# Image 0's statistics of x read through twelve buffers instead of four, group 0 kept in the ring, parameters issued by ACT, image 1's first counting moved into image 0

## The chip, the cores and the metric

The kernel runs on one core of a Trainium2 chip. The metric is the device time of the program in microseconds (us); lower is better. Times inside the program are us from the start of the profiled span.

## What is computed

```
x  [8 images, 128 channels, 256 x 256] f32
x1 = x + pointwise(shift(groupnorm(x)))          # groups of 4 channels, statistics per image
x2 = x1 + block(groupnorm(x1))                   # wavelet split, 1x1, GELU, depthwise 3x3,
                                                 # norm, two 1x1, 1x1, GELU, wavelet join
```

`shift` moves each channel by its own fraction of a pixel in y and x (four bilinear neighbours). The first group norm needs mean and variance of a whole image of x before the first row of that image can be shifted. The rest of the network does not matter here beyond this: everything behind the first layer follows it in order.

## The kernel before, in words

Channels lie on the 128 partitions. An image is cut into 32 chunks of 8 rows (1 MB, `CH` = 2048 elements per partition), taken in 8 groups (`NG`) of 4 (`SLOTS`). Every x is read twice: once for its statistics, into the four buffers `ahead[s]`, and once for the shift, into the four slots of `ring`, which hold 34 rows (one halo row above and below).

- **Counting.** DVE counts three quarters of a chunk with three `bn_stats` (`count_x`, L1056) and raises `x_counted`. ACT sums the last quarter and its squares (`sum_x`, L556 and L557) and raises `x_summed`. `load_x_ahead` (SP, L333) waits for both before it reuses a buffer, so at most four chunks are under way.
- **Scales.** `x_moments` (L1076 to 1086) joins the sums and raises `mom_ready` at L1085; PE takes the mean over the groups (`channel_means`, L767); DVE makes the variance (`group_variance`, from L1091), ACT its square root (L499), DVE the scales (`x_scales`) and from them the two scaled weight matrices (`x_weights`, L1111 and L1112), which release PE through `shift_ready`.
- **Shift.** A step of `shift_rows` on DVE handles one chunk with three passes of 128x2048: L1163 (row above), L1177 (row below, raises `u_done`), L1192 (column left, raises `v_done`). PE (`conv`) multiplies u by the weights for the column to the right (L782, needs `u_done` and x put into PSUM) and then v (L787, needs `v_done`), half a chunk at a time. ACT's step (`shift_group`) is: the next image's `sum_x`; `take_x1` of half 0 (L530, PSUM to SBUF with sums); `put_x` of the next chunk's half 0 (L508); the same for half 1, with the store of x1 (L538) between; a sum of squares (L546).
- **The next image.** While image b is shifted, DVE and ACT count image b+1, one chunk a step: group g counts group g+1 of the next image, and the last group counts group 0 of image b+2. So two things stand ahead of image 0: the statistics of image 0 (32 chunks), and the counting of group 0 of image 1 (4 chunks).
- **Orders written out by hand.** Each engine has one instruction stream, in program order. SP: 19 parameter loads (L327, all counted by `params_in`), 32 `load_x_ahead` of image 0, the four ring loads of group 0 (`load_ring`, L342), four `load_x_ahead(1, 0, s)`, then `load_image(0)`, which begins with four `load_x_ahead(1, 1, s)` and goes on with a ring load and a `load_x_ahead` per step. A ring load of slot s waits until DVE has finished u of the chunks that read the slot (`u_done`: of the next chunk too, for s < 3; of slot 3 itself for s = 3), and until ACT has put the chunk into PSUM. DVE: it waits for all parameters and for POOL's constants, does 23 small setup steps (L1022 to 1045), counts image 0, makes the moments, counts group 0 of image 1, makes the scales and starts image 0. `x_weights` comes in step 1 of image 0. ACT: sums of image 0, square root, first `put_x`, sums of group 0 of image 1, image 0. PE primes its PSUM banks after the setup and then waits for `shift_ready`.

DVE's stream between the last count of image 0 and image 0 itself reads:

```
x_moments(0, 1)
for s in range(SLOTS):
    count_x(1, 0, s)
group_variance(1, gmom_x, ps_small_x)
x_scales(1)
```

Of the kernel before, what the change touches and what calls it, by code (L numbers as in the profile page):

```python
# [45 lines left out]
def preact_kernel(nc, x, theta_s, w_dw, w_pwT, w_c1T, b_c1, bn1_g, bn1_b, dw_w, dw_b, gn_g, gn_b,  # L46
# [5 lines left out]
    with ExitStack() as ctx:  # L52
# [212 lines left out]
        cov_ready, cov_done = sem("cov_ready"), sem("cov_done")  # L265
        slot_in = [sem(f"slot_in{s}") for s in range(SLOTS)]
        ahead_in = [sem(f"ahead_in{s}") for s in range(SLOTS)]
        x1_loaded = [sem(f"x1_loaded{s}") for s in range(SLOTS)]
        bias0_ready = sem("bias0_ready")
        u_up, v_done, v_left = sem("u_up"), sem("v_done"), sem("v_left")  # L270
# [24 lines left out]
        def nth(t, back=0):  # L295

            return t + (1 + LEAD - back)

        def three_in_v(b, s):

            return final(b) and s % 2 == 1
# [21 lines left out]

        @block.sync
        def _(sp):
            for dst, src in PARAMS:
                sp.dma_start(dst, src).then_inc(params_in, 16)  # L327

            def load_x_ahead(b, g, s):

# [41 lines left out]
                    if beyond:  # L373
                        load_x_ahead(b + 2, 0, s)

            with sp.Fori(0, NG) as g:
                for s in range(SLOTS):
                    load_x_ahead(0, g, s)
            for s in range(SLOTS):
                load_ring(0, 0, s, first=True)  # L380
            for s in range(SLOTS):
                load_x_ahead(1, 0, s)
            load_image(0, before=False, tail=False, following=True, beyond=True)
            load_image(1, before=True, tail=False, following=True, beyond=True)
            with sp.Fori(2, B - 2) as b:
                load_image(b, before=True, tail=True, following=True, beyond=True)
# [103 lines left out]
        def _(act):  # L490
# [57 lines left out]
            def sum_x(b, g, s):  # L548

                q = b * NCH + g * SLOTS + s  # L550
                act.wait_ge(ahead_in[s], b * (16 * NG) + g * 16 + 16)

                wait_alone(act, nth(q, 1), x_summed)
                piece = ahead[s][:, DVE_PIECES * BANK:]
                i = g * SLOTS + s
                nc.scalar.activation(x_copy, piece, ACT.Identity, accum_out=sums_x[:, 0, bass.ds(i, 1)])  # L556
                nc.scalar.activation(x_squares, piece, ACT.Square,  # L557
                                     accum_out=sums_x[:, 1, bass.ds(i, 1)]).then_inc(x_summed, 1)
# [43 lines left out]

            def image(b, before, tail, following, beyond):

                shift_group(b, 0, before, tail, (b + 1, 1) if following else None, "first")
                with act.Fori(1, NG - 1) as g:
                    shift_group(b, g, before, tail, (b + 1, g + 1) if following else None, "")
                shift_group(b, NG - 1, before, tail, (b + 2, 0) if beyond else None, "last")

            with act.Fori(0, NG) as g:  # L610
                for s in range(SLOTS):
                    sum_x(0, g, s)
            square_root(1)
            act.wait_ge(primed, 1)
            for half in range(2):
                put_x(0, 0, 0, half)
            for s in range(SLOTS):
                sum_x(1, 0, s)
            image(0, before=False, tail=False, following=True, beyond=True)
            image(1, before=True, tail=False, following=True, beyond=True)  # L620
            with act.Fori(2, B - 2) as b:
# [363 lines left out]
        def _(dve):  # L985
# [63 lines left out]

            def count_x(b, g, s, pieces=range(DVE_PIECES)):  # L1050

                if 0 in pieces:
                    dve.wait_ge(ahead_in[s], b * (16 * NG) + g * 16 + 16)
                i = g * SLOTS + s
                for r in pieces:
                    last = nc.vector.bn_stats(stats_x[:, bass.ds(i * (6 * DVE_PIECES) + 6 * r, 6)],  # L1056
                                              ahead[s][:, r * BANK:(r + 1) * BANK])
                if DVE_PIECES - 1 in pieces:
                    last.then_inc(x_counted, 1)

# [83 lines left out]
            def shift_rows(b, g, s, before, tail, ahead_of, place):  # L1144

                t = b * NCH + g * SLOTS + s
                k = s % 2
                first, last = place == "first", place == "last"
                nx, n1 = b * 2 + 2, b * 2 + 1
                for near in range(s, min(s + 2, SLOTS)):  # L1150
                    dve.wait_ge(slot_in[near], b * (16 * NG) + g * 16 + 16)

                dve.wait_ge(conv_done, nth(t * 2 + 1, 4))
                if first and s == 0:
                    pad_columns(0)
                    done(pad_row(0))
                if first and s == 1:
                    done(pad_columns(1))
                    x_weights()
                if last and s == 0:  # L1160
                    done(pad_row(SLOTS * ROWS + 1))
                u = u_buf[k][:, :, 1:W + 1]
                stt(out=u, in0=ring[:, s * ROWS:(s + 1) * ROWS, :], scalar=up, in1=slot(s),  # L1163
                    op0=ALU.mult, op1=ALU.add).then_inc(u_up, 1)
                late = last and s == 0
                if first and s == 1:

                    dve.wait_ge(x1_ready, nth(b * (2 * NCH), 1))
                    x_bias(1 if isinstance(b, int) and b == 0 else b * 2)
                if first and s == 2 and before:  # L1170
                    group_variance(n1, gmom, ps_small)
                if last and s == 2 and not final(b):
                    group_variance(nx, gmom_x, ps_small_x)
                if ahead_of and not late:
                    count_x(*ahead_of, s, range(0, 2))
                dve.wait_ge(u_up, t + 1)
                stt(out=u, in0=ring[:, s * ROWS + 2:(s + 1) * ROWS + 2, :], scalar=down, in1=u,  # L1177
                    op0=ALU.mult, op1=ALU.add).then_inc(u_done, 1)
                if first and s == 1 and before:
                    x1_moments(b - 1)  # L1180
                if late:
                    keep_first(b)
                if ahead_of and not late:
                    count_x(*ahead_of, s, range(2, DVE_PIECES))
                if before and not three_in_v(b, s):
                    if not first:
                        count_y1(b - 1, g - 1, s)
                    elif tail:
                        count_y1(b - 2, NG - 1, s)
                dve.wait_ge(u_done, nth(t))  # L1190
                v = v_buf[k].rearrange("p (r c) -> p r c", c=W)
                left_added = stt(out=v, in0=u_buf[k][:, :, 0:W], scalar=left, in1=u, op0=ALU.mult, op1=ALU.add)  # L1192
                if three_in_v(b, s):
                    left_added.then_inc(v_left, 1)
                    if before:
                        count_y1(b - 1, g - 1, s) if not first else count_y1(b - 2, NG - 1, s)
                    dve.wait_ge(v_left, g * 2 + (s // 2 + 1))
                    stt(out=v, in0=u_buf[k][:, :, 2:W + 2], scalar=right, in1=v,
                        op0=ALU.mult, op1=ALU.add).then_inc(v_done, 1)
                else:  # L1200
                    left_added.then_inc(v_done, 1)
                if late and not final(b):
                    x_moments(b + 1, nx)
                if ahead_of and late:
                    count_x(*ahead_of, s)
                if last and s == 2 and not final(b):
                    x_scales(nx)
                if first and s == 2 and before:
                    x1_scales(n1)
                if first and s == 3 and before:  # L1210
                    c1_weights(b - 1, n1)

            def image(b, before, tail, following, beyond):

                for s in range(SLOTS):
                    shift_rows(b, 0, s, before, tail, (b + 1, 1) if following else None, "first")
                with dve.Fori(1, NG - 1) as g:
                    for s in range(SLOTS):
                        shift_rows(b, g, s, before, tail, (b + 1, g + 1) if following else None, "")
                for s in range(SLOTS):  # L1220
                    shift_rows(b, NG - 1, s, before, tail, (b + 2, 0) if beyond else None, "last")

            with dve.Fori(0, NG) as g:
                for s in range(SLOTS):
                    count_x(0, g, s)
            start_steps(SETUP_STEPS)
            x_moments(0, 1)
            for s in range(SLOTS):
                count_x(1, 0, s)
            group_variance(1, gmom_x, ps_small_x)  # L1230
            x_scales(1)
            IMAGE_STEPS = 27
            image(0, before=False, tail=False, following=True, beyond=True)
            start = SETUP_STEPS + steps[1]
# [246 lines left out]
```

## Time and profile before

| | |
|---|---|
| median of 3 runs | 5441.45 us (5440.20 to 5441.63) |
| profiled execution, its own time | 5440.21 us |
| its span, first to last instruction | 5438.6 us |
| mean granted TensorE clock | 0.964 |
| busy: PE, DVE, ACT, POOL | 88%, 86%, 77%, 19% of the span |
| HBM read, written | 946.55 MB, 662.70 MB |
| first parameter issued; first x load issued | 0.95 us; 10.33 us |
| transfers issued by ACT: stores of x1, stores of y1 | 256 of 1 MB, 128 of 512 KB |
| last chunk of image 0 counted | 96.00 us |
| first shift pass of image 0; of its group 1 | 119.56 us; 158.51 us |

The time of a run is a little more than the span, which counts from the first to the last instruction. Busy shares are over the whole program; the change touches the first 160 us or so, so the shares are read by windows and by the timeline.

### The profile page before, as it was taken

To read this page: it belongs to the slowest core of one execution; us is meant where nothing else is said; L and a number is where in the kernel's file an instruction comes from. 1 tells how busy PE (TensorE), PEld (TensorE's weight loads), DVE (VectorE), ACT (ScalarE), POOL (GpSimd) and SP (SyncE) were. 2 spreads that over 40 slices of the span, in tenths; PEclk is the share of its full clock that TensorE was granted. 3 is DMA by queue.
4 is the path that set the end of the run, shared out by engine and by line. 5 is a ranking of instruction groups with operands and counts; after the bars stand their busy time and mean duration, and the time that the engine had idled before them with its cause. 6 is when DMAs were issued, how large, how long until landed. Compare 5 with 4: busy or idle time off the path is not lost.

```text
span 5438.6 us, 54871 instructions
## 1 busy us (share of the span) xinstructions
PE 4778.1 (88%) x12740; PEld 2174.6 (40%) x12740; DVE 4686.9 (86%) x4430; ACT 4166.8 (77%) x5706; POOL 1047.0 (19%) x743
## 2 busy tenths in 40 slices
PE   0889999999999999999998999999997777777775
PEld 0334444444444444444443555555552222222222
DVE  6999898898988989889937999999659888888887
ACT  4887777777777777777736788888659888888887
POOL 0000000000000000000004888888501111111111
PEclk6999999999999999999999999999999999999998
DMA  8999999999999999999993333333239999999999
GB/s 346 363 358 411 426 425 425 416 426 426 415 426 416 426 426 417 426 397 373 398 330 125 124 128 128 132 130 129 75 76 221 235 236 236 236 235 236 236 236 223
DMA packets 256302, 1610.79 MB, mean 296 GB/s; under 512 B 30256, under 2 KB 30640, under 8 KB 92336
## 3 DMA queue, kind: packets, MB, share of 16 engines
q1 hardware_dynamic: 164016, 1005.35, 46.8%
q0 software_dynamic: 36864, 268.45, 23.8%
q10 hardware_dynamic: 55296, 335.57, 14.8%
q8 instruction: 48, 0.79, 0.1%
q14 instruction: 78, 0.64, 0.0%
HBM read 946.55 MB, written 662.70 MB: 296 GB/s over the span
## 4 chain that ended last, share of the span: by engine, by line
PE 43%; DMA 23%; DVE 17%; issue 9%; ACT 4%; DVEq 0%; ACTq 0%; POOLq 0%; SPq 0%; POOL 0%
DMA out_x<-arena 19%; PE ps L799 14%; PE ps L787 11%; PE ps L782 10%; PE ps L870 4%; DMA arena<-in_x 3%; DVE arena L1290 2%; DVE arena L1177 2%; ACT arena L744 2%; DVE arena L1314 2%; DVE arena L1163 2%; PE ps L917 2%; DVE arena L1192 2%; DVE arena L1427 2%; DVE ps L1303 1%
## 5 line engine op out<-in xcount | busy, mean ns | idle before, releaser
L972 PE MATMUL ps<-arena,c2T 128*128 128x512 f32 x2048 | 1025.9, 652 | 365.9 <-ACT arena L737 363.6
L787 PE MATMUL ps<-arena 128*128 128x512 f32 x2048 | 964.4, 595 | 24.4 <-DVE arena L1192 24.4
L799 PE MATMUL ps<-arena 128*128 128x512 f32 x2048 | 963.7, 614 | 15.2 <-DVE small L1141 13.1
L782 PE MATMUL ps<-arena 128*128 128x512 f32 x1920 | 913.0, 598 | 42.9 <-DVE arena L1112 22.9
L453 POOL TENSOR_SCALAR arena<-arena,taps 128x1024 f32<-128x1024 f32 x238 | 265.9, 1117 | 2914.5 <-ACT arena L650 2882.0
L530 ACT ACTIVATE arena<-ps,small 128x1024 f32<-128x1024 f32 x512 | 567.6, 1109 | 321.5 <-PE ps L787 320.9
L972 PEld LDWEIGHTS ps<-arena,c2T 128*128 128x128 f32 x2048 | 401.5, 205 | 989.6 <-ACT arena L737 560.9
L737 ACT ACTIVATE arena<-ps,small 128x512 f32<-128x512 f32 x1024 | 713.1, 778 | 99.8 <-DVE arena L1419 91.1
L1163 DVE SCALAR_TENSOR_TENSOR arena<-arena,shift 128x2048 f32<-128x2048 f32 x256 | 601.2, 2348 | 199.8 <-DMA arena<-in_x 149.9
L1303 DVE SCALAR_TENSOR_TENSOR ps<-arena,taps,ps 128x512 f32<-128x512 f32 (+1 forms) x604 | 683.2, 1177 | 21.3 <-PE ps L917 20.7
L508 ACT ACTIVATE ps<-arena 128x1024 f32<-128x1024 f32 x512 | 526.3, 1028 | 169.5 <-ACT arena L530 159.6
L1177 DVE SCALAR_TENSOR_TENSOR arena<-arena,shift 128x2048 f32<-128x2048 f32 x256 | 598.2, 2337 | 1.4
L799 PEld LDWEIGHTS ps<-arena 128*128 128x128 f32 x2048 | 383.1, 189 | 540.8 <-issue 534.8
L787 PEld LDWEIGHTS ps<-arena 128*128 128x128 f32 x2048 | 386.9, 190 | 529.6 <-issue 475.4
L1192 DVE SCALAR_TENSOR_TENSOR arena<-arena,shift 128x2048 f32<-128x2048 f32 x256 | 597.8, 2335 | 0.6
L744 ACT ACTIVATE arena<-arena 128x2048 f32<-128x2048 f32 x256 | 490.1, 1915 | 112.6 <-DVE arena L1427 110.7
L782 PEld LDWEIGHTS ps<-arena 128*128 128x128 f32 x1920 | 360.8, 190 | 521.6 <-issue 448.3
L1056 DVE BATCH_NORM_STATS2 arena<-arena 128x512 f32 (+1 forms) x768 | 498.9, 682 | 29.7 <-DMA arena<-in_x 29.4
L1426 DVE TENSOR_TENSOR arena<-arena 128x1024 f32<-128x1024 f32 x256 | 314.4, 1228 | 209.9 <-DMA out_x<-arena 208.7
L546 ACT ACTIVATE arena<-arena 128x2048 bf16<-128x2048 f32 x256 | 484.8, 1894 | 0.4 <-ACT arena L530 0.4
L481 POOL DMA_DIRECT2D out_x<-arena x256 | 218.1, 852 | 1321.8 <-ACT arena L744 1288.5
L467 POOL TENSOR_TENSOR arena<-arena 128x1024 f32<-128x1024 f32 x128 | 302.5, 2364 | 129.6 <-ACT arena L686 70.8
(167 smaller groups left out, 5409.3 us busy)
## 6 DMA issues: line engine op xcount, KB each, us to landing
arena<-in_x SPq DMA_DIRECT2D x400, 1024.0 KB, 16.0
out_x<-arena ACTq DMA_DIRECT2D x256, 1024.0 KB, 9.0
arena<-out_x SPq DMA_DIRECT2D x256, 1024.0 KB, 17.0
out_x<-arena POOLq DMA_DIRECT2D x256, 1024.0 KB, 17.0
arena<-in_x SPq DMA_DIRECT2D x112, 1152.0 KB, 15.5
y_dram<-arena ACTq DMA_DIRECT2D x128, 512.0 KB, 8.6
arena<-y_dram SPq DMA_DIRECT2D x128, 512.0 KB, 3.6
h_dram<-arena SPq DMA_DIRECT2D x112, 512.0 KB, 2.7
```

The lines of the kernel that those rows point to most:

```text
L508: nc.scalar.activation(banks(half), ring[:, bass.ds(1 + s * ROWS + half * 4, 4), :] .rearrange("p r c -> p (r c)"), ACT.Copy).then_inc(x_i ...
L530: nc.scalar.activation(x1_buf[k][:, half * (CH // 2):(half + 1) * (CH // 2)], banks(half), ACT.Identity, bias=bias0, accum_out=total).then ...
L737: last = nc.scalar.activation(g_buf[k][:, q, :], ps[:, 4 * k + q, :], ACT.Gelu, bias=z_bias[:, q:q + 1], scale=z_scale[:, q:q + 1])
L744: nc.scalar.activation(y_buf[s], y_buf[s], ACT.Copy, scale=0.5).then_inc(y_ready, 1)
L782: mm(ps[:, r, :], w_right[:, :], u_buf[k][:, 2 * r:2 * r + 2, 2:W + 2], start=False, stop=False, skip_group_check=True)
L787: last = mm(ps[:, r, :], w_center[:, :], v_buf[k][:, r * BANK:(r + 1) * BANK], start=False, stop=True, skip_group_check=True)
L799: last = mm(ps[:, 4 + s % 2, :], w_c1b[:, q, :], cells[:, q // 2, q % 2, :, :], start=(q == 0), stop=(q == 3))
L972: last = mm(ps[:, 4 * k + q, :], c2T[:, q, :], h2[:, k * HC:(k + 1) * HC], start=True, stop=True)
L1163: stt(out=u, in0=ring[:, s * ROWS:(s + 1) * ROWS, :], scalar=up, in1=slot(s), op0=ALU.mult, op1=ALU.add).then_inc(u_up, 1)
L1177: stt(out=u, in0=ring[:, s * ROWS + 2:(s + 1) * ROWS + 2, :], scalar=down, in1=u, op0=ALU.mult, op1=ALU.add).then_inc(u_done, 1)
L1192: left_added = stt(out=v, in0=u_buf[k][:, :, 0:W], scalar=left, in1=u, op0=ALU.mult, op1=ALU.add)
L1303: stt(out=acc, in0=h_tile(t, dy, dx, first), scalar=tap_weight(dy, dx), in1=acc, op0=ALU.mult, op1=ALU.add).then_inc(dw_acc, 1)
```

## The change

- SP no longer issues the parameters; ACT issues the same 19 transfers ahead of its first `sum_x`. SP begins with x.
- The 32 chunks of image 0 go to twelve buffers. Group 0 is loaded into the ring's slots, counted there and stays for the shift. Odd groups go to `ahead[s]`, even groups from 2 on to `x1_in[s]`, which image 0 does not use otherwise, with new semaphores `first_in[s]`. From group 3 on a load waits until the chunk 8 places before it has been counted by DVE and ACT. The later reload of the ring's group 0 is gone.
- The loops over image 0's chunks are unrolled on SP, ACT and DVE.
- Group 0 of image 1 is counted in the steps of group 0 of image 0. Group 1 of image 1 is counted in a block of its own between group 0 and group 1 of image 0, four chunks on DVE and four on ACT. From group 1 on all is as before.
- SP's order at that place is: ring(0, 1, s) and ahead(1, 1, s) in turn for four s, then ahead(1, 2, s) for four s, then as before.
- For image 0, `x_weights` stands right behind `x_scales`, ahead of step 0.

```diff
@@ helpers
+        def first_chunk(g, s):
+            if g == 0:
+                return slot(s).rearrange("p r c -> p (r c)"), slot_in[s], 16
+            return (ahead[s], ahead_in[s], g * 8 + 8) if g % 2 else (x1_in[s], first_in[s], g * 8)
+
+        def ahead_count(b, g):
+            return b * (16 * NG) + g * 16 + (16 - 16 * (NG // 2))
@@ SP
-            for dst, src in PARAMS:
-                sp.dma_start(dst, src).then_inc(params_in, 16)
...
-            with sp.Fori(0, NG) as g:
-                for s in range(SLOTS):
-                    load_x_ahead(0, g, s)
-            for s in range(SLOTS):
-                load_ring(0, 0, s, first=True)
+            def load_first_image():
+                for s in range(SLOTS):
+                    load_ring(0, 1, s)
+                    load_x_ahead(1, 1, s)
+                for s in range(SLOTS):
+                    load_x_ahead(1, 2, s)
+                with sp.Fori(2, NG - 1) as g:
+                    for s in range(SLOTS):
+                        load_ring(0, g, s)
+                        load_x_ahead(1, g + 1, s)
+                for s in range(SLOTS):
+                    load_ring(0, NG - 1, s, last=True)
+                    load_x_ahead(2, 0, s)
+
+            for t in range(NCH):
+                g, s = t // SLOTS, t % SLOTS
+                if g == 0:
+                    load_ring(0, 0, s, first=True)
+                    continue
+                chunk, arrived, _ = first_chunk(g, s)
+                if g > 2:
+                    wait_alone(sp, nth(t, 2 * SLOTS), x_counted, x_summed)
+                sp.dma_start(chunk, x[0, :, t * CH:(t + 1) * CH]).then_inc(arrived, 16)
             for s in range(SLOTS):
                 load_x_ahead(1, 0, s)
-            load_image(0, before=False, tail=False, following=True, beyond=True)
+            load_first_image()
@@ ACT
-                shift_group(b, 0, before, tail, (b + 1, 1) if following else None, "first")
+                first_image = isinstance(b, int) and b == 0
+                shift_group(b, 0, before, tail, (b + 1, 0 if first_image else 1) if following else None, "first")
+                if first_image:
+                    for s in range(SLOTS):
+                        sum_x(1, 1, s)
...
-            with act.Fori(0, NG) as g:
-                for s in range(SLOTS):
-                    sum_x(0, g, s)
+            for dst, src in PARAMS:
+                act.dma_start(dst, src).then_inc(params_in, 16)
+            for t in range(NCH):
+                sum_x(0, t // SLOTS, t % SLOTS)
             square_root(1)
             act.wait_ge(primed, 1)
             for half in range(2):
                 put_x(0, 0, 0, half)
-            for s in range(SLOTS):
-                sum_x(1, 0, s)
@@ DVE
                 if first and s == 1:
                     done(pad_columns(1))
-                    x_weights()
+                    if not (isinstance(b, int) and b == 0):
+                        x_weights()
...
-                    shift_rows(b, 0, s, before, tail, (b + 1, 1) if following else None, "first")
+                    shift_rows(b, 0, s, before, tail, (b + 1, 0 if first_image else 1) if following else None, "first")
+                if first_image:
+                    for s in range(SLOTS):
+                        count_x(1, 1, s)
...
-            with dve.Fori(0, NG) as g:
-                for s in range(SLOTS):
-                    count_x(0, g, s)
+            for t in range(NCH):
+                count_x(0, t // SLOTS, t % SLOTS)
             start_steps(SETUP_STEPS)
             x_moments(0, 1)
-            for s in range(SLOTS):
-                count_x(1, 0, s)
             group_variance(1, gmom_x, ps_small_x)
             x_scales(1)
+            x_weights()
```

`sum_x` and `count_x` take buffer, semaphore and count from `first_chunk` for image 0 and the count from `ahead_count` for the others.

## Rows read from the trace of the kernel before

**Rows 1.** Windows of core 0: us, busy of each engine (count), granted clock, DMA share, GB/s.

```profile
50.00:75.00 25.00, 0.00 (x0) 0.00 (x0) 18.94 (x32) 16.40 (x45) 0.00 (x0) 0.50 1.01 421
...
175.00:200.00 25.00, 21.59 (x48) 8.61 (x48) 25.00 (x19) 22.30 (x36) 0.00 (x0) 1.00 0.99 368
...
600.00:800.00 200.00, 198.52 (x461) 86.20 (x461) 182.88 (x178) 154.33 (x247) 0.00 (x0) 1.00 1.01 425
```

**Rows 2.** Timeline, first 40 us: start, length, engine, line, operation, [idle before <-releaser].

```profile
0.95 0.39 SPq L327 DMA_DIRECT2D theta<-in_theta_s  x1
...
9.45 0.43 SPq L327 DMA_DIRECT2D bn<-in_bn_b  x1
10.33 29.91 SPq L333 DMA_DIRECT2D arena<-in_x  x13
11.49 0.15 DVE L1022 TENSOR_SCALAR small<-theta 128x1 f32<-128x1 f32 x1 [11.49 <-DMA bn<-in_bn_b]
...
15.65 1.28 ACT L556 ACT_TABLE_LOAD   x1 [15.65 <-DMA arena<-in_x]
...
18.82 7.22 DVE L1056 BATCH_NORM_STATS2 arena<-arena 128x512 f32 x12 [0.35 <-DVE gram L1045]
```

**Rows 3.** Timeline, 85 to 140 us, from the last counted chunk to the first output.

```profile
94.12 1.88 DVE L1056 BATCH_NORM_STATS2 arena<-arena 128x512 f32 x3 [0.61 <-DMA arena<-in_x]
...
99.41 0.16 DVE L1085 SCALAR_TENSOR_TENSOR small<-small,part 128x2 f32<-128x2 f32 x1
...
115.94 0.14 DVE L1091 COPY small<-ps 128x2 f32<-128x2 f32 x1
...
119.56 2.35 DVE L1163 SCALAR_TENSOR_TENSOR arena<-arena,shift 128x2048 f32<-128x2048 f32 x1
...
132.27 3.78 PE L782 MATMUL ps<-arena 128*128 128x512 f32 x4 [12.68 <-DVE arena L1112]
...
137.84 1.11 ACT L530 ACTIVATE arena<-ps,small 128x1024 f32<-128x1024 f32 x1 [11.37 <-PE ps L787]
```

**Rows 4.** Chain of waits in order of time, 86 to 160 us: start, length, what.

```profile
120.14 4.86 DMA arena<-in_x
...
136.05 1.75 PE ps L787 x4
...
149.95 2.34 DVE arena L1163
...
158.51 2.34 DVE arena L1163
```

**Rows 5.** Parameter transfers (L327), issued 1 to 10 us: time to landing.

```profile
DMA to landing us min/median/max: 1.9/2.1/2.8
```

**Rows 6.** DMA queues in 802.5 to 804.5 us, image 1: packets, MB, share of 16 engines.

```profile
q1 hardware_dynamic: 76, 0.55, 65.1%
q10 hardware_dynamic: 77, 0.32, 38.3%
```

**Rows 7.** The page, DMA queues over the whole span: packets, MB, share of 16 engines.

```profile
q10 hardware_dynamic: 55296, 335.57, 14.8%
```

**Rows 8.** Loads of 512 KB on SP, 2900:4000 alone, 4300:5300 beside q0: landing.

```profile
arena<-y_dram SPq DMA_DIRECT2D x122, 512.0 KB, 3.6
...
q0 software_dynamic: 25916, 188.72, 90.8%
q1 hardware_dynamic: 12954, 47.17, 12.5%
...
arena<-h_dram SPq DMA_DIRECT2D x90, 512.0 KB, 10.2
```

**Rows 9.** ACT in the timeline at 161.65 us: the fourth sum of group 0.

```profile
161.65 0.61 ACT L556 ACTIVATE arena<-arena 128x512 bf16<-128x512 f32 x1
```

**Rows 10.** L333 loads issued at 148.0 and at 163.2 us: time to landing.

```profile
DMA to landing us min/median/max: 8.1/8.1/8.1
...
DMA to landing us min/median/max: 12.7/12.7/12.7
```

More of the change, by code:

```diff
@@ L267, in preact_kernel @@
         ahead_in = [sem(f"ahead_in{s}") for s in range(SLOTS)]
+        first_in = [sem(f"first_in{s}") for s in range(SLOTS)]
         x1_loaded = [sem(f"x1_loaded{s}") for s in range(SLOTS)]
@@ L550, in sum_x @@
                 q = b * NCH + g * SLOTS + s
-                act.wait_ge(ahead_in[s], b * (16 * NG) + g * 16 + 16)
+                chunk, arrived, count = first_chunk(g, s) if isinstance(b, int) and b == 0 else \
+                    (ahead[s], ahead_in[s], ahead_count(b, g))
+                act.wait_ge(arrived, count)
                 wait_alone(act, nth(q, 1), x_summed)
-                piece = ahead[s][:, DVE_PIECES * BANK:]
+                piece = chunk[:, DVE_PIECES * BANK:]
                 i = g * SLOTS + s
@@ L1050, in count_x @@
             def count_x(b, g, s, pieces=range(DVE_PIECES)):
+                chunk, arrived, count = first_chunk(g, s) if isinstance(b, int) and b == 0 else \
+                    (ahead[s], ahead_in[s], ahead_count(b, g))
                 if 0 in pieces:
-                    dve.wait_ge(ahead_in[s], b * (16 * NG) + g * 16 + 16)
+                    dve.wait_ge(arrived, count)
                 i = g * SLOTS + s
@@ L1056, in count_x @@
                     last = nc.vector.bn_stats(stats_x[:, bass.ds(i * (6 * DVE_PIECES) + 6 * r, 6)],
-                                              ahead[s][:, r * BANK:(r + 1) * BANK])
+                                              chunk[:, r * BANK:(r + 1) * BANK])
                 if DVE_PIECES - 1 in pieces:
@@ L1213, in image @@
             def image(b, before, tail, following, beyond):
+                first_image = isinstance(b, int) and b == 0
                 for s in range(SLOTS):
-                    shift_rows(b, 0, s, before, tail, (b + 1, 1) if following else None, "first")
+                    shift_rows(b, 0, s, before, tail, (b + 1, 0 if first_image else 1) if following else None, "first")
+                if first_image:
+                    for s in range(SLOTS):
+                        count_x(1, 1, s)
                 with dve.Fori(1, NG - 1) as g:
```

## The prediction, written before the changed kernel had run

> **What bounds the kernel now.** I read the windows first. While image 0 is counted, the DMA engines are full (share 1.01, 421 GB/s) and DVE works 18.94 of 25 us; while it is shifted, DVE is busy 25.00 of 25 us; from image 1 on the DMA is full again and sets the pace [rows 1]. Every later stage follows the end of the head in order, with the same transfers and buffers, so what the head gains or loses I carry to the end one for one. The head is read in the timeline. SP issues its first x at 10.33 us, behind 19 parameters issued from 0.95 us at 0.47 us each; DVE leaves the wait for the parameters at 11.49 us, sets up for 7.33 us and begins to count at 18.82 us [rows 2]. The last chunk is counted at 94.12 + 1.88 = 96.00 us, the moments are out at 99.57 us. Then DVE waits for four chunks of image 1 and counts them, and the variance comes only at 115.94 us, the first shift pass at 119.56 us [rows 3]. Step 0 then waits until 125.00 us for a load issued at 120.14 us; group 1 of image 0 begins at 158.51 us [rows 4]. I forecast that last mark; call it G1.
>
> **The order behind the count.** T0 is the first shift pass. After the change it follows the last count by: moments 99.57 - 96.00 = 3.57; PE's group mean and its hand-over, which no row of mine shows alone, 0.7 (not under 0.1, and not over the 0.95 of one cold matmul record of 512 columns, 3.78 / 4 [rows 3], as it has two columns); variance, root, scales and pads 119.56 - 115.94 = 3.62 [rows 3]; the two weight matrices, each 128x128, 0.4 (under one 128x512 count of 0.60, 7.22 / 12 [rows 2], apiece). That is 8.3 us, where it took 23.56. So the order by itself gives back 15.3 us: the reload of ring and image 1's counting have left the path.
>
> **From T0 to G1.** Before: 158.51 - 119.56 = 38.95 us. Steps are 8.56 us (158.51 - 149.95 [rows 4]). After: four steps and 0.7 of pads and bias, 34.9 us, without the wait for the load (image 1's group 0 is issued as image 0's last group is counted, and has all of the 8.3 us and 2.4 more). Then the new block of four counts on DVE, 4 x 3 x 0.60 = 7.2 us. That would be G1 = T0 + 42.1. But look at who lets the fourth chunk of it be loaded. Load ahead(1, 1, 3) waits for ACT's sum of (1, 0, 3), the first thing in ACT's step 3. ACT's first drain comes 5.9 us (two passes and two counts) after T0 for u, then 3.78 us of cold matmuls and 1.75 us of warm ones [rows 3, 4]: T0 + 11.4. From first drain to the fourth sum it took 161.65 - 137.84 = 23.8 us, the sum itself 1.2 [rows 3, 9]; with some waits for v instead of a backlog I take 26. So the load is issued at T0 + 37.5, when DVE stands at 34.9. Ahead of it on SP's queue are ring(0, 1, 2), ahead(1, 1, 2) and ring(0, 1, 3), all let go at the end of step 3, beside a store of x1. Such loads took 8.1 us from issue to landing with little before them and 12.7 in just this crowd [rows 10]; I take 10.5. It lands at T0 + 48, is counted in 1.9: G1 = T0 + 50, with ends 46.5 and 52.5, and 42.1 only if the load came without wait. Compared with 38.95 this half loses 11 us of the 15.3.
>
> **The start of the stream.** Moving the parameters lets x start about 9 us sooner: first issue near 1.3 instead of 10.33. If nothing else happened, the stream would end near 87 us instead of 94.1: earlier by 9.0, less some 2 us for parameter bytes and packets that now share the engines. DVE needs 32 x 1.805 = 57.8 us for its counts, so it stays hidden if it begins by about 30, which asks for the parameters by 23 us. They land within 2.8 us of issue now, with empty queues [rows 5]. Issued by ACT from about 1.5 to 10 us, they meet twelve 1 MB loads that SP issues in the same 6 us without any wait. What do the engines do then? They are spared this by the twelve buffers running out: after 12 x 2.49 us (1 MB at 421 GB/s [rows 1]) there is no x left to load until DVE counts, and DVE counts nothing until the parameters are in. First landing 1.3 + 5.3 (15.65 - 10.33 [rows 2]), the twelfth 27.4 later, 2 for the parameters between, 1 to 2 for the seven left over: the parameters are in at about 37 us, not 11.49.
>
> The Trainium skill ("DMA: Bandwidth & Descriptors", Queues, rings and completion order) says that an engine drains a whole packet of 9 to 17 descriptors from one queue before it turns to the next. Equal bursts would fit rows 6 too; with 17 of the small against 9 of the large, the parameters would be in some 7 us sooner, and the sum below would be that much lower. The sum goes by one for one.
>
> Then: setup 7.33, DVE starts at 44.3. Chunk 12 waits for five chunks counted (44.3 + 9.0), is issued at 53.6 and lands 5 to 6 us later, 59. Nineteen more at 2.49: 106.3. Counted: 108.2 us, against 96.0. The DVE bound, 44.3 + 57.8 = 102.1, lies below. So the new start costs 12.2 us where it was to give 8. ACT's own sums (1.5 us a chunk against 2.49) and PE's priming stay covered.
>
> **Sum.** T0 = 108.2 + 8.3 = 116.5. G1 = 166.5, against 158.51: 8.0 us later. Behind G1: ahead(1, 2, 0) is issued near T0 + 46 and wanted at T0 + 52.4; with 5 us it lands at 51, at no cost. The profiled execution goes from 5440.21 to 5448.2; it lies 1.24 us below the median of the three runs, from which the same sum gives 5449.4. I say 5449. What the measurement can tell from no change is about 0.2%, 10.9 us, so this is no change by that bound. Its own range: parameters 33 to 39, landing 8.1 to 12.7, gives 5443 to 5455.
>
> **Rivals.**
> 1. *Parameters pass quickly.* If small packets slip through, or the first of them get ahead of the x loads and the rest take a few us, they are in before 23 us; DVE is hidden, the last chunk is counted at 88, T0 = 96.3, G1 = 146.3: 12 us faster, 5429. For it: they land in 2 us now [rows 5]. Against it: rows 6 and 8. Chance 0.20. If the fourth load also cost nothing, 5421.
> 2. *Late parameters, no stall at the fourth load.* G1 = 116.5 + 42.1 = 158.6, 5441 to 5443. For it: the DMA has slack in the steps before, while 34.9 against 37.5 is a narrow gap on ACT. Against it: the 12.7 of rows 10. Chance 0.17.
> 3. *The stall goes on into group 1.* The block's sums on ACT let go ahead(1, 2, 0) only at T0 + 46; if it too takes 12.7 us behind the fourth load and the store of chunk 3, it lands at 58.7 where DVE wants it at 52.4. Price 6.3 us, so 14 in all: 5456. It decides once that landing takes more than 6.4 us. For it: both landings of rows 10 are longer than that. Against it: by then nothing else of SP's is queued, since ring(0, 2, 0) waits for step 1 of group 1. Chance 0.14.
> 4. *The change does not do what it says.* Twelve buffers bring nothing to the rate, as the DMA is full with four [rows 1]; that is in the sum already.
>
> **How the numbers follow.** The forecast gets 0.47, rivals 1 to 3 get 0.20, 0.17 and 0.14; 0.02 is elsewhere. The range goes from 5428, to take in most of rival 1, to 5456, to take in rival 3. Faster by over 0.2% (below 5430.6): rival 1 and a little, 0.21. Slower by over 0.2% (above 5452.3): rival 3 and the top end of the forecast, 0.20. The rest is 0.59: forecast and rival 2.
>
> **What would show it.** Right: first DVE setup step (L1022 before) near 37 us instead of 11.49, idle on the parameters; a hole in DMA from about 37 to 54 us; last chunk of image 0 counted near 108; first shift pass near 116; a DVE wait of 5 to 8 us for x in the block between groups 0 and 1; G1 near 166. Wrong: a first setup step before 23 us, and the last count near 88 us; or a block that takes 7.2 us flat. If G1's shift is not the shift of the end, the idea that the DMA-bound images carry it one for one is wrong.

## The result and the profile after

The changed kernel takes 5456.11 us (median of 9 runs, 5449.55 to 5457.76) against 5441.63 (9 runs, 5436.00 to 5446.03) for the kernel before: ratio 1.0025, 95% interval 1.0015 to 1.0036. It is slower by 14.5 us between the medians. The forecast was 5449 with a range up to 5456, so the median lies at the very top of the range, and beyond the 0.2% inside which I had put most of the chance. The profiled execution took 5452.45 us, span 5450.8, that is 12.2 us more than before. Three executions in the slow state, two of e2 (6375 and 8127 us) and one of e4 (9230 us), are left out of the ratios below.

The marks of the forecast, read in both traces and in those of the experiments. "Setup" is DVE's first setup step, "counted" the end of the last count of image 0, T0 the first shift pass, G1 the first shift pass of group 1.

| kernel | setup | counted | T0 | G1 | G1 - T0 | span |
|---|---|---|---|---|---|---|
| before | 11.49 | 96.00 | 119.56 | 158.51 | 38.95 | 5438.6 |
| forecast for the change | 37 | 108.2 | 116.5 | 166.5 | 50 | |
| after | 38.60 | 109.96 | 118.20 | 171.60 | 53.40 | 5450.8 |
| e1, parameters on SP | 11.49 | 94.8 | 103.05 | 157.62 | 54.57 | 5437.2 |
| e2, setup late | late | 98.6 | 106.85 | 159.90 | 53.05 | 5439.1 |
| e3, block in x1_in | 38.73 | 109.7 | 117.98 | 159.84 | 41.86 | 5437.9 |
| e4, before with parameters on ACT | 19.22 | 103.6 | 127.18 | 166.43 | 39.25 | 5448.2 |
| e5, e1 and e3 | 11.50 | 94.8 | 103.02 | 144.89 | 41.87 | 5425.0 |
| e6, spread, late, x1_in | late | 91.5 | 99.75 | 141.62 | 41.87 | 5422.6 |
| e7, half packets | 39.16 | 112.4 | 120.66 | 174.52 | 53.86 | 5455.9 |
| e8, weights late | 38.81 | 110.0 | 117.84 | 172.79 | 54.95 | 5454.5 |
| e9, ahead first | 38.73 | 110.3 | 118.48 | 164.92 | 46.44 | 5451.0 |
| e10, as e6, setup earlier | late | 90.3 | 98.54 | 140.41 | 41.87 | 5419.6 |

("Counted" is the start of the aggregation of the moments less 0.31 us, its distance from the last count in the kernels before and after. "Late": the setup stands behind chunk 20 or 23. The marks are of one profiled execution each.)

The span moves with G1 to within some 2 us in every kernel but one: in e9 G1 is 6.4 us later than in the kernel before and the end 12.4, because a further wait of 4.4 us stands behind G1.

**The start.** The timeline of the kernel after, first 60 us, answers to [rows 2]:

```profile
2.04 0.41 ACTq L644 DMA_DIRECT2D theta<-in_theta_s  x1
...
7.04 1.80 ACTq L644 DMA_DIRECT2D gn<-in_gn_g  x1
...
11.43 3.48 ACTq L644 DMA_DIRECT2D pw1T<-in_pw_wT  x1
...
31.06 2.21 ACTq L644 DMA_DIRECT2D bn<-in_bn_b  x1
33.41 1.28 ACT L585 ACT_TABLE_LOAD   x1 [33.41 <-issue]
...
38.60 0.15 DVE L1054 TENSOR_SCALAR small<-theta 128x1 f32<-128x1 f32 x1 [38.60 <-DMA bn<-in_bn_b]
...
45.62 14.93 DVE L1090 BATCH_NORM_STATS2 arena<-arena 128x6 f32<-128x512 f32 x25
```

SP issues x at 1.43 us, but DVE's first setup step waits until 38.60 us for the last parameter. The first nine of ACT's issues take 0.4 to 0.9 us each; from the tenth on all but one take 1.8 to 6.5 us, and ACT's first sum, with its table load, comes at 33.41. The DMA view of 2 to 40 us gives the time from issue to landing:

```profile
arena<-in_w_c1T ACTq DMA_DIRECT2D x1, 256.0 KB, 15.3
...
theta<-in_theta_s ACTq DMA_DIRECT2D x1, 1.0 KB, 7.6
wdw<-in_w_dw ACTq DMA_DIRECT2D x1, 0.5 KB, 10.1
...
taps<-in_dw_w ACTq DMA_DIRECT2D x1, 4.5 KB, 23.4
...
gn<-in_gn_b ACTq DMA_DIRECT2D x1, 0.5 KB, 27.7
...
bn<-in_bn_b ACTq DMA_DIRECT2D x1, 2.0 KB, 7.5
```

These answer to [rows 5], where none took over 2.8 us. Issue and landing time together put theta at 9.6 us, the second parameter at 12.6, the fourth at 19.2, the eighth (taps) at 29.4: 2.5 to 3.5 us apart, where I had put 2.8. The eleventh is in at 36.6, the last at 38.6. And the two queues between 20 and 30 us, for [rows 6]:

```profile
q1 hardware_dynamic: 566, 4.13, 99.4%
q10 hardware_dynamic: 565, 0.01, 3.4%
```

566 packets against 565, while the one moves 4.13 MB and the other 0.01. The hole in the DMA that I had forecast from 37 to 54 us comes as well, until SP issues the next x load (chunk 12) at 54.72 us:

```profile
40.00:50.00 10.00, 4.36 (x5) 1.85 (x6) 9.41 (x34) 9.19 (x29) 0.00 (x0) 1.00 0.01 2
```

**Behind the count**, for [rows 3]:

```profile
108.08 1.88 DVE L1090 BATCH_NORM_STATS2 arena<-arena 128x6 f32<-128x512 f32 x3 [0.60 <-DMA arena<-in_x]
...
114.21 0.16 DVE L1125 COPY small<-ps 128x2 f32<-128x2 f32 x1 [0.68 <-PE ps L799]
...
118.20 2.35 DVE L1198 SCALAR_TENSOR_TENSOR arena<-arena,shift 128x2048 f32<-128x2048 f32 x1
```

From the last count (109.96) to T0 8.24 us.

**The block between groups 0 and 1**, in the timeline and, below it, the landing of the load issued at 155.92 us, for [rows 10]:

```profile
150.19 0.33 SPq L349 DMA_DIRECT2D arena<-in_x  x1
...
151.03 0.33 SPq L340 DMA_DIRECT2D arena<-in_x  x1
...
152.94 3.65 DVE L1090 BATCH_NORM_STATS2 arena<-arena 128x6 f32<-128x512 f32 x6
...
155.92 16.19 SPq L340 DMA_DIRECT2D arena<-in_x  x5
...
162.17 1.88 DVE L1090 BATCH_NORM_STATS2 arena<-arena 128x6 f32<-128x512 f32 x3 [5.58 <-DMA arena<-in_x]
...
169.80 1.88 DVE L1090 BATCH_NORM_STATS2 arena<-arena 128x6 f32<-128x512 f32 x3 [5.75 <-DMA arena<-in_x]
...
171.60 2.34 DVE L1198 SCALAR_TENSOR_TENSOR arena<-arena,shift 128x2048 f32<-128x2048 f32 x1
...
173.85 1.28 DVE L1090 BATCH_NORM_STATS2 arena<-arena 128x512 f32 x2
```

```profile
DMA to landing us min/median/max: 13.9/13.9/13.9
```

DVE counts two chunks at once, waits 5.58 us for the third and 5.75 for the fourth, which was issued at T0 + 37.7 and took 13.9 us to land. Group 1 itself has no such wait. The windows of that stretch, for [rows 1]:

```profile
155.00:160.00 5.00, 3.49 (x9) 1.22 (x7) 1.58 (x3) 4.17 (x9) 0.00 (x0) 1.00 1.00 405
160.00:165.00 5.00, 0.00 (x0) 0.00 (x0) 1.88 (x3) 4.75 (x9) 0.00 (x0) 0.57 1.01 429
165.00:170.00 5.00, 0.00 (x0) 0.00 (x0) 0.20 (x1) 2.18 (x9) 0.00 (x0) 0.50 1.00 423
```

The DMA is full for all 15 us and DVE works 3.66 of them.

### The profile page after: what moved, and what is told of

It is laid out like the page before. It is cut to its first block, busy times and chain, and to the rows that moved or that the text cites. A ratio compares the mean times of both kernels' runs of the same rounds, so it can differ in the third digit from the quotient of the medians.

```text
span 5450.8 us, 54465 instructions
## 1 busy us (share of the span) xinstructions
PE 4783.9 (88%) x12740; PEld 2177.6 (40%) x12740; DVE 4684.9 (86%) x4430; ACT 4156.7 (76%) x5699; POOL 1046.9 (19%) x743
## 3 DMA queue, kind: packets, MB, share of 16 engines
q1 hardware_dynamic: 160704, 1000.41, 46.4%
## 4 chain that ended last, share of the span: by engine, by line
PE 42%; DMA 24%; DVE 19%; issue 10%; ACT 3%; ACTq 1%; DVEq 0%; POOLq 0%; SPq 0%; POOL 0%
DMA out_x<-arena 19%; PE ps L831 13%; PE ps L819 10%; PE ps L814 10%; DMA arena<-in_x 4%; PE ps L902 4%; DVE arena L1212 3%; DVE arena L1327 2%; DVE arena L1198 2%; DVE arena L1351 2%; ACT arena L776 2%; DVE arena L1090 2%; PE ps L949 2%; DVE arena L1464 2%; DVE arena L1227 2%
## 5 line engine op out<-in xcount | busy, mean ns | idle before, releaser
L1340 DVE SCALAR_TENSOR_TENSOR ps<-arena,taps,ps 128x512 f32<-128x512 f32 (+1 forms) x604 | 686.2, 1189 | 21.5 <-PE ps L949 20.8
```

Source lines behind the costliest of these rows:

```text
L1340: stt(out=acc, in0=h_tile(t, dy, dx, first), scalar=tap_weight(dy, dx), in1=acc, op0=ALU.mult, op1=ALU.add).then_inc(dw_acc, 1)
```

## The experiments

### e1: the parameters back on SP

```diff
+            for dst, src in PARAMS:                       # SP, ahead of x
+                sp.dma_start(dst, src).then_inc(params_in, 16)
-            for dst, src in PARAMS:                       # ACT
-                act.dma_start(dst, src).then_inc(params_in, 16)
```

> The changed kernel with one part undone: the 19 parameters are issued by SP ahead of x again. Theory (parameters queued behind twelve x loads, one packet for one): first setup step of DVE back at 11.5 us instead of 38.6, x begins at 10.4, last chunk of image 0 counted near 95 instead of 109.96, first shift pass near 103, group 1 of image 0 near 156.5 instead of 171.6. End about 15 us below the changed kernel, about 2 us below the kernel before: 5440. Rival (the parameters do not matter, the late load of the block does): as the changed kernel, 5456.

Measured: 5439.13 us against 5442.83 for the kernel before, run beside it, ratio 0.9994 (0.9985 to 1.0003). The start is back where it was; the stall of the block remains. DVE's timeline:

```profile
11.49 0.15 DVE L1055 TENSOR_SCALAR small<-theta 128x1 f32<-128x1 f32 x1 [11.49 <-DMA bn<-in_bn_b]
...
95.12 2.75 DVE L1115 BATCH_NORM_AGGREGATE small<-arena 128x2 f32<-128x576 f32 x1
...
103.05 2.35 DVE L1199 SCALAR_TENSOR_TENSOR arena<-arena,shift 128x2048 f32<-128x2048 f32 x1
```

```profile
155.82 1.88 DVE L1091 BATCH_NORM_STATS2 arena<-arena 128x6 f32<-128x512 f32 x3 [5.77 <-DMA arena<-in_x]
157.62 2.33 DVE L1199 SCALAR_TENSOR_TENSOR arena<-arena,shift 128x2048 f32<-128x2048 f32 x1
```

T0 is 15.15 us earlier than in the changed kernel, from this one edit, and G1 14.0. This edit alone takes the changed kernel from slower to level with the kernel before (so does e3, by another term).

### e2: DVE counts first and sets up after chunk 23

```diff
-            dve.wait_ge(params_in, 16 * len(PARAMS))
...
             for t in range(NCH):
+                if t == 24:
+                    set_up()
                 count_x(0, t // SLOTS, t % SLOTS)
```

`set_up()` holds the wait for the parameters and the 23 setup steps.

> The changed kernel, but DVE counts first and does its parameter setup only after chunk 23, so that DVE no longer waits for the parameters. Theory A (DVE's wait is the only damage): x never pauses, last count near 89, group 1 at 150.6, end 21 us below the changed kernel: 5435. Theory B (ACT is held as well, because it cannot issue its 19 transfers while the engines are full, and its first sum comes at 33 us or later): x pauses after twelve chunks until ACT has summed five, chunk 12 is issued near 42, last count near 96.5, group 1 near 158, end 13 us below the changed kernel: 5442 to 5444. I hold B for likelier.

Measured: 5443.71 us, ratio 1.0001 (0.9992 to 1.001). Theory B: DVE no longer waits for a parameter, and still a hole comes, from ACT. DVE's timeline around it, and SP's loads issued from 30 to 60 us:

```profile
37.15 1.88 DVE L1092 BATCH_NORM_STATS2 arena<-arena 128x6 f32<-128x512 f32 x3 [0.88 <-DMA arena<-in_x]
46.96 1.88 DVE L1092 BATCH_NORM_STATS2 arena<-arena 128x6 f32<-128x512 f32 x3 [7.93 <-DMA arena<-in_x]
```

```profile
L407 SPq DMA_DIRECT2D arena<-in_x x12: 327/328/328, 42.1 to 58.0; - x12
```

Chunk 12 is issued at 42.1 (forecast 42), after ACT has at last summed five. So the changed kernel is held twice by the parameters: DVE by their landing, ACT by their issue; mending DVE alone gives back 11.7 us of G1's 13.1 and not the 21 that theory A asked for.

### e3: group 1 of image 1 in the idle x1_in buffers

```diff
             for s in range(SLOTS):
                 load_x_ahead(1, 0, s)
+            for s in range(SLOTS):
+                sp.dma_start(x1_in[s], x[1, :, (SLOTS + s) * CH:(SLOTS + s + 1) * CH]).then_inc(first_in[s], 16)
@@ load_first_image
                     load_ring(0, 1, s)
-                    load_x_ahead(1, 1, s)
-                for s in range(SLOTS):
                     load_x_ahead(1, 2, s)
```

The block and `sum_x(1, 1, s)` read `x1_in[s]`; the counts of `ahead_in` behind it are 16 lower.

> The changed kernel, but group 1 of image 1 is loaded into the four x1_in buffers, right behind group 0 of image 1 and before image 0 starts, so the block between groups 0 and 1 finds its data. Theory (the block waits for its third and fourth load): first shift pass unchanged near 118.2, the block takes 7.3 us without a wait, group 1 at T0 + 42.1 = 160.3 instead of 171.6; end 11 us below the changed kernel: 5445. Rival (DMA is short in group 0 anyway and the wait moves to the loads of group 2): group 1 starts at 160 but DVE waits in it, end within 4 us of the changed kernel.

Measured: 5441.55 us, ratio 0.9999 (0.999 to 1.0008); 14.6 us below the changed kernel by the medians, 11.8 by G1, 12.9 by the span. The block, and the first step of group 1 behind it:

```profile
152.72 7.21 DVE L1094 BATCH_NORM_STATS2 arena<-arena 128x6 f32<-128x512 f32 x12
159.84 2.33 DVE L1202 SCALAR_TENSOR_TENSOR arena<-arena,shift 128x2048 f32<-128x2048 f32 x1
162.10 1.28 DVE L1094 BATCH_NORM_STATS2 arena<-arena 128x512 f32 x2
```

No wait in the block and none moved into group 1: the rival falls.

### e4: the kernel before with its parameters on ACT

```diff
-            for dst, src in PARAMS:                       # SP
-                sp.dma_start(dst, src).then_inc(params_in, 16)
+            for dst, src in PARAMS:                       # ACT, ahead of its sums
+                act.dma_start(dst, src).then_inc(params_in, 16)
```

x still goes through four buffers.

> The kernel before with one part of the change alone: the parameters issued by ACT. Only four x loads can be under way. Theory (one packet for one while x is queued, then free): four x loads are done at about 14 us, the parameters are in at about 17 us, DVE counts from about 24.5 instead of 18.82, chunk 4 is issued at 26.5, last count near 100.5 instead of 96.0; end 4 to 5 us above the kernel before: 5446. Rival (small transfers pass quickly): parameters in by 12 to 13 us, last count 95 to 96.5, end within 1 us of the kernel before.

Measured: 5449.20 us against 5442.83, ratio 1.0013 (1.0004 to 1.0022), span 9.6 us over that of the kernel before. The parameters come at 19.22 us (forecast 17), G1 at 166.43 (7.9 us late, where 4.5 was forecast).

```profile
19.22 0.15 DVE L1021 TENSOR_SCALAR small<-theta 128x1 f32<-128x1 f32 x1 [19.22 <-DMA bn<-in_bn_b]
```

One part of the change alone, put into the old kernel, costs 6 to 10 us. The direction is the theory's; its size was set too low: I let the parameters behind the four x loads pass in 3 us, and the last of them is issued only at 15.64 us and takes 3.6 us to land.
### e5: e1 and e3 together

```diff
+                sp.dma_start(dst, src).then_inc(params_in, 16)          # as in e1
+                sp.dma_start(x1_in[s], x[1, :, (SLOTS + s) * CH:(SLOTS + s + 1) * CH]).then_inc(first_in[s], 16)   # as in e3
```

> Both repairs together: parameters on SP ahead of x, and group 1 of image 1 in the x1_in buffers. Theory (the two damages are separate terms that add): first shift pass at 103.1 as with the parameters on SP alone, group 1 at T0 + 42.0 = 145.1, which is 13.4 us ahead of the kernel before; end 5428 to 5430, ratio 0.9975. Rival (they hide one another): end no better than 5436.

Measured: 5427.76 us against 5442.81, ratio 0.9973 (0.9964 to 0.9982). T0 at 103.02, G1 at 144.89 (forecast 145.1). The terms add to within 1 us: e1 takes 14.0 us off G1, e3 11.8, both 26.7.

### e6: parameters one by one between ACT's sums, setup late, x1_in

The edits of e2 and e3, and:

```diff
             for t in range(NCH):
+                if t < len(PARAMS):
+                    act.dma_start(*PARAMS[t]).then_inc(params_in, 16)
                 sum_x(0, t // SLOTS, t % SLOTS)
```

> As the previous run, but the parameters stay on ACT, one issued ahead of each of its first 19 sums, and DVE does its setup after chunk 23. Theory (neither ACT nor DVE waits for a parameter while x flows): x from 1.4 us without a pause, last count near 89, first shift pass near 97.1, group 1 near 139.1, 19 us ahead of the kernel before; end 5422 to 5424. Rival (small transfers beside x cost more than they save): last count after 94, end 5428 or more.

Measured: 5423.74 us against 5442.81, ratio 0.9965 (0.9951 to 0.9979). The time is in the range, the marks are 2.6 us late (T0 99.75, not 97.1). DVE's timeline says why: behind the setup its last eight counts run as one row without a wait,

```profile
68.40 1.88 DVE L1096 BATCH_NORM_STATS2 arena<-arena 128x6 f32<-128x512 f32 x3 [0.61 <-DMA arena<-in_x]
...
77.18 14.34 DVE L1096 BATCH_NORM_STATS2 arena<-arena 128x6 f32<-128x512 f32 x24
```

so the end of the count is DVE's there and not the data's. ACT's issues take 0.33 to 0.40 us each, none is held.

### e7: x in half packets

```diff
-                sp.dma_start(chunk, x[0, :, t * CH:(t + 1) * CH]).then_inc(arrived, 16)
+                sp.dma_start(chunk[:, 0:CH // 2], x[0, :, t * CH:t * CH + CH // 2]).then_inc(half_in[g % 2][s], 16)
+                sp.dma_start(chunk[:, CH // 2:CH], x[0, :, t * CH + CH // 2:(t + 1) * CH]).then_inc(arrived, 16)
```

> The changed kernel, but chunks 4 to 31 of image 0 are loaded as two halves of 4 KB per partition each, so from the fifth chunk on the x packets are half as large and twice as many. In the changed kernel the parameters behind the first few land 2.5 us apart. Theory (one packet for one): behind the first four chunks they land 1.4 to 1.6 us apart and ACT's slow issues shrink in the same ratio; the parameters are in at 32 to 36 us instead of 38.6. Rival (shared by bytes or by time): the spacing does not shrink, parameters in at 38 us or later.

There is one execution: 5457.51 us. The two queues between 20 and 30 us, and two of ACT's issues:

```profile
q1 hardware_dynamic: 1040, 3.79, 96.0%
q10 hardware_dynamic: 1043, 0.10, 8.4%
```

```profile
15.49 1.11 ACTq L648 DMA_DIRECT2D pw2T<-in_pw_wT  x1
16.64 1.10 ACTq L648 DMA_DIRECT2D bpw<-in_pw_b  x1
```

### e8: the weights back in step 1

```diff
-                    if not (isinstance(b, int) and b == 0):
-                        x_weights()
+                    x_weights()
...
             x_scales(1)
-            x_weights()
```

> The changed kernel with x_weights back in step 1 of image 0. Theory (the load of (1, 1, 3) waits for ACT's sum of (1, 0, 3), which follows PE's start): PE starts at T0 + 12.6 instead of T0 + 5.9, ACT's first drain 6 us later, that load is issued near T0 + 43.5 instead of 37.7, group 1 starts near T0 + 59 instead of T0 + 53.4; end 4 to 6 us above the changed kernel. Rival (DMA alone sets the landing, not the issue): group 1 within 1.5 us of T0 + 53.4.

Measured: 5455.32 us, ratio 1.0022 (1.0013 to 1.0032), which cannot be told from the changed kernel. SP's issue of ring(0, 1, 2) and of the fourth chunk's load, DVE's step 2 and the first pass of group 1:

```profile
151.33 0.33 SPq L349 DMA_DIRECT2D arena<-in_x  x1
...
158.59 14.71 SPq L340 DMA_DIRECT2D arena<-in_x  x5
```

```profile
136.93 2.35 DVE L1197 SCALAR_TENSOR_TENSOR arena<-arena,shift 128x2048 f32<-128x2048 f32 x1 [1.01 <-PE ps L819]
...
172.79 2.33 DVE L1197 SCALAR_TENSOR_TENSOR arena<-arena,shift 128x2048 f32<-128x2048 f32 x1
```

In the changed kernel PE starts at T0 + 5.9 and ACT's first drain at T0 + 12.5; here at T0 + 9.5 and T0 + 15.6. (My 12.6 and 6 us were read off the kernel before, whose step 0 held a wait of 3.1 us for a load; that was the error.) The load is issued at T0 + 40.8 instead of 37.7, so ACT's 3.1 us pass on to the issue in full, which is the theory's part. But the load lands in 12.4 us instead of 13.9, and G1 comes at T0 + 54.95, 0.05 us outside what the rival allowed and far from the theory's 59. The 1.55 us that are left need no late issue: DVE itself begins the last pass of step 3 1.5 us later (T0 + 33.98 instead of 32.49), as `x_weights` stands in step 1 and step 2 waits 1.01 us for PE, and ring(0, 1, 2), the first of the loads in front of the fourth, is issued 1.5 us later too (T0 + 33.5 instead of 32.0). Counted from that first issue, the landing does not follow the issue of the fourth load. In us, for the seven traces in which these loads stand in this order:

| kernel | ring(0, 1, 2) issued | fourth load issued, after that | landed, after that |
|---|---|---|---|
| before | 155.91 | 7.3 | 20.0 |
| e4 | 164.24 | 6.9 | 19.4 |
| after | 150.19 | 5.7 | 19.6 |
| e1 | 135.04 | 5.7 | 20.8 |
| e2 | 138.84 | 5.7 | 19.3 |
| e7 | 152.65 | 5.6 | 20.1 |
| e8 | 151.33 | 7.3 | 19.7 |

("Landed" is issue plus landing time in the kernel before and e4, where nothing waits for this load, and the start of DVE's fourth count in the others.) The DMA is full all the while (share 0.98 or more in each half of the stretch), and what is queued from the end of step 3 on sets the landing: with the fourth load issued 5.6 to 7.3 us behind the first, no trace shows an effect of its own of the moment at which ACT lets it go. The early weights, one of the change's parts, gave some 1.2 us at G1 in these two traces, and nothing that the medians show.

### e9: the ahead load before the ring load

```diff
-                    load_ring(0, 1, s)
                     load_x_ahead(1, 1, s)
+                    load_ring(0, 1, s)
```

> The changed kernel, with load ahead(1, 1, s) ahead of ring(0, 1, s) in SP's stream in the first group. Theory (the third and fourth load are late because of what stands before them in SP's queue, and only the fourth because of ACT): the third load is issued near T0 + 29 instead of T0 + 32.8 and lands in time, so its wait of 5.6 us in the block is gone; the fourth is still issued near T0 + 37.5 but without ring(0, 1, 3) before it and lands near T0 + 47; group 1 at T0 + 49 instead of T0 + 53.4; end 4 to 5 us below the changed kernel. Rival (the DMA as a whole is full there, whatever the order): group 1 within 1.5 us of T0 + 53.4, and waits for ring in group 1 if not.

Measured: 5452.47 us against 5442.24, ratio 1.0017 (1.0008 to 1.0026). G1 comes 6.7 us earlier than in the changed kernel (T0 + 46.4, where the theory had 49), but the end only 3.6 by the medians and not at all by the spans, where 4 to 5 were forecast. DVE's timeline:

```profile
163.12 1.88 DVE L1090 BATCH_NORM_STATS2 arena<-arena 128x6 f32<-128x512 f32 x3 [4.47 <-DMA arena<-in_x]
164.92 2.34 DVE L1198 SCALAR_TENSOR_TENSOR arena<-arena,shift 128x2048 f32<-128x2048 f32 x1
171.66 1.28 DVE L1090 BATCH_NORM_STATS2 arena<-arena 128x512 f32 x2 [4.41 <-DMA arena<-in_x]
...
177.97 2.35 DVE L1198 SCALAR_TENSOR_TENSOR arena<-arena,shift 128x2048 f32<-128x2048 f32 x1
```

The third load's wait is gone, and the fourth's is 4.47 us; but step 0 of group 1 now waits 4.41 us for (1, 2, 0), and step 1 starts at 177.97 against 180.15 in the changed kernel. Queue order moves the wait; with the DMA full from 155 to 175 us (share 1.00) it removes only 2.2 us of it. Theory and rival are both right in part. e3, which loads those 4 MB before image 0, removes it all.

### e10: as e6, with the setup after chunk 20

```diff
-                if t == 24:
+                if t == 21:
                     set_up()
```

> As the run with spread parameters and late setup, but the setup stands after chunk 20 instead of chunk 23. There the last eight counts ran back to back on DVE behind the setup and ended at 91.52, later than the data. Theory (those are DVE's, not DMA's): the last count ends near 89.8, first shift pass near 98.0, group 1 near 140.0; end 1.5 to 2 us below the 5423.7 of that run. Rival (the last parameters are not in by then and DVE waits): a DVE wait for a parameter before the setup, end above 5424.

Measured: 5421.98 us against 5442.24, ratio 0.9963 (0.995 to 0.9977), span 19.0 us below that of the kernel before. T0 at 98.54 (1.2 us earlier than e6; 98.0 forecast), G1 at 140.41 (140.0). The ten chunks behind the setup are counted without a wait, and the last one waits 0.60 us for its data, so DVE has just caught up with the stream:

```profile
69.89 17.94 DVE L1096 BATCH_NORM_STATS2 arena<-arena 128x6 f32<-128x512 f32 x30
88.43 1.88 DVE L1096 BATCH_NORM_STATS2 arena<-arena 128x6 f32<-128x512 f32 x3 [0.60 <-DMA arena<-in_x]
```

This is the fastest version tried, 20.3 us below the kernel before beside it; from e6 it is 1.8 us by the medians, with times that overlap (5419.96 to 5423.02 against 5421.21 to 5424.26).

## Why the prediction was right or wrong

**Parameters behind x: right, a little small.** "The parameters are in at about 37 us": 38.60. "Chunk 12 ... issued at 53.6": issued at 54.72, with DVE's first count at 45.62 (44.3). Last count 109.96 against 108.2. Setup 7.02 us to the first count. e1 gives all of it back, e7 shows equal packet counts at another packet size. One step had it too short without effect: SP was to issue the twelve loads in 6 us without a wait, and took from 1.43 to 10.35 us.

The rule of the Trainium skill that I weighed ("DMA: Bandwidth & Descriptors", Queues, rings and completion order: bursts of 9 to 17 descriptors) did not come out apart. Equal counts fit single packets and equal bursts alike, and the 7 us less that I had estimated for unequal bursts did not appear (38.60 us against 37).

**The order behind the count: right.** 8.24 us against 8.3.

**Steps and block without waits: right.** 42.1 forecast, 41.86 in e3, e5, e6 and e10.

**The wait in the block: foreseen, its landing mis-sized.** The step "I take 10.5" for the landing of ahead(1, 1, 3) failed: it was issued at T0 + 37.7 (forecast 37.5) and took 13.9 us, beyond both rows that I had bounded it with. That is 3.4 us and the whole miss of G1 - T0. Of the two rows the 12.7 was the like case: that load stood behind three loads issued in the 7.3 us before it, as here behind three in 5.7 us (the four are 4.2 MB, beside stores of x1). The 8.1 had one load issued just before it. I took the middle between the two. And a landing added to an issue is the wrong form for this term: by e8 and its table the landing follows the start of the crowd, at 19.3 to 20.8 us, and not ACT's sum. I had also overlooked that the third load waits (5.58 us); it cost nothing beyond the fourth's.

That the issue came out at 37.5 against 37.7 is in part luck: ACT's first drain comes at T0 + 12.5 and not 11.4, and from there to the issue it takes 25.2 us and not 26. The ends that I gave, 46.5 and 52.5, do not follow from landings of 8.1 and 12.7, which give 47.5 and 52.1; nor does 5455 for the upper end of the sum, which comes to 5454.

**The sum.** Forecast +8.0 at G1, measured +13.1: 1.7 from the start (118.20 against 116.5), 3.4 from the landing. The span carries 12.2 of it to the end and the medians 14.5; the profiled execution is one of the shorter ones of the nine. That the shift of G1 passes on one for one holds to some 2 us in all kernels but e9.

**The rivals.** Rival 1 (parameters pass quickly) and rival 2 (no stall) did not come. Rival 3 gave the time that was measured, 5456, by another way: group 1 of the changed kernel has no wait for (1, 2, 0). That wait exists, 4.41 us, but only in e9, where the fourth load comes early enough to uncover it. Rival 4 is borne out as far as e1 shows it: with the parameters on SP, twelve buffers end the count at 94.8 us against 96.0. The chance that I gave to "slower by over 0.2%", 0.20, was too low for a forecast whose own upper end was 5455.

## What to carry to other kernels

Before deepening a prefetch, look at what else is on the DMA at that time and who waits for it: put the small, needed transfers ahead of the flood (e1), or give them slack by moving their consumer back and their issue apart (e6, e10). And a counting step moved between two groups needs its data loaded before the crowd, not in it: an idle buffer was worth 11.8 us, a better queue order 2.2.

## What was not expected of the hardware

- Issuing is held, not only landing. ACT's first nine issues took 0.41 to 0.93 us, the tenth 1.80 and most later ones 2.2 to 6.5, while x loads stood in the other queue; spread between sums, 0.33 to 0.40 (e6). SP shows the same in e7, where the eleventh of its issues takes 1.12 us and the thirteenth 3.12. In e2 this alone kept ACT's first sum until 34.9 us and left DVE 7.93 us without x.
- The last eight parameters landed within about 2 us once x had run dry, after eleven had taken 34. So most of the time of the first eleven was waiting for turns.
